# Moving the loads of the stacked Q and K pieces from the SP queue to GpSimd's queue

## The reference

```
L0:  xn  = layernorm(x) * (1 + scale(t)) + shift(t)          scale, shift from the step's embedding
     q,k,v = xn@Wq+bq, xn@Wk+bk, xn@Wv+bv                    16 heads of 16
     s   = q k^T / 4 + attention_bias ; s = -inf where masked; p = softmax(s)
     x1  = xn + (p v)@Wo + bo
     x   = x1 + gelu2(layernorm(x1)*g2+beta2 @ W1 + b1) @ W2 + b2
L1, L3: down projection to 64, gelu, expert matrix chosen per batch element, up projection, residual, layernorm
L2:  rotation of neighbouring features by theta and phi
```

## Time and profile before

| | |
|---|---|
| median of 3 runs | 1190.88 us (1186.92 to 1195.05) |
| profiled execution | 1190.11 us, span 1188.2 us |
| granted TensorE clock | 0.954 |
| busy: PE, DVE, ACT, POOL | 1038.0 (87%), 819.3 (69%), 782.7 (66%), 350.5 (29%) us |
| transfers | 209.41 MB, mean 176 GB/s |

### The profile page before, as it was taken

How to read it: one execution, slowest core, us unless ns; L and a number is a source line. 1 busy time by engine, 2 the same in 40 slices (tenths; PEclk the granted TensorE clock), 3 DMA queues, 4 the chain that set the end, 5 groups by cost and what they waited for, 6 DMA issues and landing times. The chain is left out here.

```text
span 1188.2 us, 22037 instructions
## 1 busy us (share of the span) xinstructions
PE 1038.0 (87%) x6042; PEld 668.8 (56%) x6128; DVE 819.3 (69%) x2056; ACT 782.7 (66%) x1238; POOL 350.5 (29%) x464
## 2 busy tenths in 40 slices
PE   2689999989989989989999999795699998898863
PEld 2446556545645555645654565453577776776641
DVE  5666786776767667758667675674546788978665
ACT  2477887877778778768777786674445656656432
POOL 0205115113212221411511321001555456645421
PEclk9889999999999999999998999898799999999966
DMA  6576986977895896796797696843111101101001
GB/s 229 182 251 203 317 250 217 319 210 237 266 277 187 249 316 219 204 313 217 229 315 212 227 275 172 296 145 121 39 36 36 36 18 53 44 27 36 18 18 36
DMA packets 119913, 209.41 MB, mean 176 GB/s; under 512 B 19104, under 2 KB 46624, under 8 KB 115744
## 3 DMA queue, kind: packets, MB, share of 16 engines
q1 hardware_dynamic: 119840, 208.63, 55.9%
HBM read 187.62 MB, written 20.97 MB: 176 GB/s over the span
## 5 line engine op out<-in xcount | busy, mean ns | idle before, releaser
L690 DVE CUSTOM_DVE_ANT_0 prob<-s_bank,big 128x512 f32<-128x512 f32 x512 | 346.0, 688 | 178.7 <-PE s_bank L549 127.4
L835 ACT ACTIVATE prob<-prob,nmax 128x512 f32<-128x512 f32 x512 | 363.9, 724 | 80.1 <-DVE nmax L690 75.9
L558 PEld LDWEIGHTS t_bank<-ident,prob 128*128 128x128 f32 x2048 | 240.3, 142 | 212.2 <-issue 80.8
L558 PE MATMUL t_bank<-ident,prob 128*128 128x128 f32 x2048 | 320.9, 280 | 10.9 <-ACT prob L835 4.6
L842 ACT COPY pt<-t_bank 128x512 f32<-128x512 f32 x320 | 184.9, 578 | 93.2 <-PE t_bank L558 90.7
L548 PE MATMUL s_bank<-stack_k,stack_q 128*128 128x512 bf16 x426 | 163.9, 385 | 28.1 <-DVE nmax L690 28.1
L549 PE MATMUL s_bank<-mterm_early,ident_bf 128*128 128x512 bf16 x448 | 172.0, 384 | 6.5 <-DMA stack_k<-pieces_dram 2.1
L699 DVE COPY pt<-t_bank 128x512 f32<-128x512 f32 x192 | 132.2, 688 | 41.1 <-PE t_bank L558 41.1
L571 PE MATMUL o_bank<-pt,val 128*32 128x512 f32 x1024 | 140.3, 623 | 0.7 <-ACT pt L842 0.7
L1639 POOL TENSOR_TENSOR gl<-big,gh 128x512 fp32r<-128x512 f32 x64 | 87.2, 1373 | 86.7 <-DVE gh L1344 86.7
L954 POOL TENSOR_SCALAR val<-vst 128x64 f32<-128x64 f32 x128 | 27.0, 244 | 287.7 <-PE o_bank L571 250.1
(11 more groups left out here) (176 smaller groups left out, 1624.1 us busy)
## 6 DMA issues: line engine op xcount, KB each, us to landing
big<-in_fside_Bx16xSxS SPq DMA_DIRECT2D x128, 1024.0 KB, 6.7
stack_q<-pieces_dram SPq DMA_DIRECT2D x128, 128.0 KB, 5.4
stack_k<-pieces_dram SPq DMA_DIRECT2D x128, 128.0 KB, 5.0
pieces_dram<-pieces SPq DMA_DIRECT2D x32, 384.0 KB, 7.1
xin<-in_x SPq DMA_DIRECT2D x8, 512.0 KB, 6.0
x_dram<-x SPq DMA_DIRECT2D x8, 512.0 KB, 3.0
big<-x_dram SPq DMA_DIRECT2D x8, 512.0 KB, 3.3
x1r<-x_dram SPq DMA_DIRECT2D x8, 512.0 KB, 4.4
```

The lines of the kernel that those rows point to most:

```text
L558: last = pe.transpose(t_bank[n % 2][:, c * P:(c + 1) * P], prob[:, n % NT, c * P:(c + 1) * P], ident[:])
L690: dve.tensor_tensor_reduce(out=prob[:, n % NT, :], in0=s_bank[n % 3][:, :], in1=bias[:, h % NB, t, :], scale=-1.0, scalar=3e38, op0=ALU.ad ...
L835: act.activation(tile, tile, ACT.Exp, bias=nmax[:, n % NT:n % NT + 1], scale=-1.0).then_inc(exped.sem, 1)
```

## The change

`load_stack` moves from SP's program to GpSimd's. It now issues one load of Q and one of K per call, and is called behind eight steps in a row: for half 0 behind steps 42 to 49 of the same iteration, for half 1 behind steps 4 to 11 of the next. In the prologue all 16 loads of half 0 come before the first copies of the values, and the 16 of half 1 after them. The waits are the same as before, on GpSimd's queue. SP keeps the stores of the pieces and all other transfers, in their old order.

```diff
--- before.py
+++ after.py
@@ -214,7 +214,8 @@
 TWO_PI_PARTS = (_c1, _c2, 2 * np.pi - _c1 - _c2)
 
 
-HEADS_OF_LOADS = dict(x1=2, expert=4, mask=5, store_0=7, store_1=11, stack_0=9)
+HEADS_OF_LOADS = dict(x1=2, expert=4, mask=5, store_0=7, store_1=11)
+STACKS_FROM = (42, 4)
 STATISTICS_AT, DEVIATION_AT, NORMALISE_AT = 11, 12, 14
 WEIGH_AFTER = 17
 CONTEXT_AFTER = 21
@@ -440,19 +441,6 @@
                     apart(sp, sp_apart)
                     sp.dma_start(pieces_dram[:, qk, c], pieces[:, qk, :, :]).then_inc(pieces_out[c][qk].sem, 16)
 
-            def load_stack(b, c, first=False):
-                if not first:
-
-                    sp.wait_ge(scored.sem, scored.at(b, STEPS // 2 * (c + 1)))
-                    apart(sp, sp_apart)
-                for qk, (stack, piece) in enumerate(((stack_q, QPIECE), (stack_k, KPIECE))):
-                    sp.wait_ge(pieces_out[c][qk].sem, pieces_out[c][qk].at(b, 16))
-                    apart(sp, sp_apart)
-                    for i in range(NP8):
-                        src = pieces_dram[:, qk, c, piece[i]].rearrange("(e h) t -> e h t", e=HD)
-                        sp.dma_start(stack[i::NP8, c * HC:(c + 1) * HC], src
-                                     ).then_inc(stack_in[c].sem, 16)
-
             def store_x1(b):
                 sp.wait_ge(x1_done.sem, x1_done.at(b, DC))
                 apart(sp, sp_apart)
@@ -493,14 +481,9 @@
                         store_pieces(b, 0)
                     if h == HEADS_OF_LOADS["store_1"] and not last:
                         store_pieces(b, 1)
-                    if h == HEADS_OF_LOADS["stack_0"] and not last:
-                        load_stack(b, 0)
-                if not last:
-                    load_stack(b, 1)
 
             for c in range(DC):
                 store_pieces(-1, c, first=True)
-                load_stack(-1, c, first=True)
                 if c == 0:
                     load_x(0)
             iteration(0, first=True)
@@ -974,6 +957,17 @@
                     mterm_late[:, t, :], mraw[:, t, :], MASKED, 0.0, ALU.mult, ALU.add
                 ).then_inc(late_term.sem, 1)
 
+            def load_stack(b, c, i, first=False):
+                if i == 0 and not first:
+
+                    pool.wait_ge(scored.sem, scored.at(b, STEPS // 2 * (c + 1)))
+                for qk, (stack, piece) in enumerate(((stack_q, QPIECE), (stack_k, KPIECE))):
+                    if i == 0:
+                        pool.wait_ge(pieces_out[c][qk].sem, pieces_out[c][qk].at(b, 16))
+                        apart(pool, pool_apart)
+                    src = pieces_dram[:, qk, c, piece[i]].rearrange("(e h) t -> e h t", e=HD)
+                    pool.dma_start(stack[i::NP8, c * HC:(c + 1) * HC], src).then_inc(stack_in[c].sem, 16)
+
             def keep_residual(b, first=False):
                 pool.wait_ge(xt_done.sem, xt_done.at(b, DC))
                 if not first:
@@ -987,6 +981,10 @@
                         copy_values(b - 1, NG - 1)
                     if n == RESIDUAL_AT and not first:
                         keep_residual(b - 1)
+                    if not last and 0 <= n - STACKS_FROM[0] < NP8:
+                        load_stack(b, 0, n - STACKS_FROM[0])
+                    if not first and 0 <= n - STACKS_FROM[1] < NP8:
+                        load_stack(b - 1, 1, n - STACKS_FROM[1])
                     if not last and n in CUT_STEPS:
                         cut(b, CUT_STEPS.index(n))
                     if not last and n in VALUES_AT:
@@ -1001,8 +999,12 @@
             for t in range(QT):
                 early_mask_term(-1, t, first=True)
             pool.wait_ge(consts, 3)
+            for i in range(NP8):
+                load_stack(-1, 0, i, first=True)
             for g in range(NG):
                 copy_values(-1, g, first=True)
+            for i in range(NP8):
+                load_stack(-1, 1, i, first=True)
             keep_residual(-1, first=True)
             iteration(0, first=True)
             before = links[0]
```

## The result

The changed kernel takes 1195.16 us (median of 20 runs, 1191.54 to 1200.28), the kernel before 1191.25 beside it: a ratio of 1.0036 [1.0023, 1.0049]. The forecast was 1178. The time went up by 4 us instead of down by 13. The profiled execution of after took 1200.28 us, 5.1 above its median (span 1198.4, mean clock 0.949 against 0.954), so its traces overstate the difference: 10.2 us between the spans.

The account below looks back on a forecast made before the run. TensorE was busy 95 of 100 us; late transfers cost only by stopping TensorE, VectorE or ScalarE. From 1190.11 us, +6.9 - 3.3 + 3 - 11.5 - 7.5 = -12.4 gave 1178; 8-in-10 range 1162 to 1205.

Parts of the forecast that it names:

- Part 6: Loop's jump back: with two stack loads there instead of sixteen, five stalls each shrink 1.5 us, -7.5 (0 to -26).
- Part 5: Last iteration: SP's late loads start earlier, the bias of head 4 lands in time, with clock gain -11.5 us.
- The floor of 1.5: Jump back: guessed shortest stall, 1.5 us, for a free instruction fetch; no row supported it.
- The 1.6 us of clock: Jump back: TensorE's clock at 0.59 over 4 us after the pause, a loss of 1.6 us each that might be recovered.
- the sign by which the prediction was to fall: Prediction falls altogether if TensorE waits for the stack at step 61, or late loads still delay the last iteration's bias.
- Part 1: GpSimd's queue: price of issuing one stack load, taken as 0.95 us, with ends 0.6 and 1.3.
- c: Time GpSimd needs to issue one stack load, forecast 0.95 us, ends 0.6 and 1.3.
- Rival (b): GpSimd issues as quickly as SP, 0.63 us a load: 1170 us; chance 0.18.
- (a): GpSimd issues slowly, 1.16 us a load, so VectorE waits for the residual copy: 1199 us; chance 0.20.
- (d): GpSimd's descriptors wait for VectorE's SBUF-only work, up to 4 us in each of six iterations: 1202 us; chance 0.05.
- Part 2: Prologue: fifteen issues in a row delay first scores, +6.9 us; SP freed, iteration 0's bias wait goes, -3.3.
- Parts 3 and 4: Loop: half-0 issues at steps 42 to 49 hidden; half-1 at steps 4 to 11 tight, allowance +3 us over six iterations.

Follow-up runs that it names:

- a_from6: Changed kernel with GpSimd's half-1 stack loads behind steps 6 to 13 instead of 4 to 11: 1185.40 us, 0.9949 of the kernel before.
- b_spread: Kernel before, with the 21 late loads spread three each behind heads 5 to 11 of the last iteration: 1181.42 us, ratio 0.9922.
- a_spread: Changed kernel with the 21 late loads spread over heads 5 to 11 of the last iteration: 1188.63 us, 0.9976 of the kernel before.
- a_stack16: Changed kernel with GpSimd's half-1 stack loads from step 16 on instead of step 4: 1186.10 us, 0.9966 of the kernel before.
- a_pro: Changed kernel with SP waiting in the prologue for stack 0 before loading x and storing the second pieces: 1192.32 us, 1.0021 of the kernel before.
- a_best: Changed kernel with half-1 stack loads behind steps 6 to 13, late loads spread, SP waiting for stack 0 in the prologue: 1177.51 us, 0.9886 of before.
- b_xearly: Kernel before, with SP's load of x issued ahead of the 16 half-1 stack loads instead of behind: 1196.28 us, ratio 1.0039.
- a_nobias: Changed kernel without the bias loads after the first four heads, whose bias is used again: 1162.82 us, one run.

## Why the prediction was wrong

Against the profiled executions, forecast and trace by stretch:

| stretch | forecast | trace |
|---|---|---|
| to the first jump back | +6.9 - 3.3 - 1.5 + 0.5 = +2.6 | -0.5 |
| first to last jump back | -4 x 1.5 + 4 x 0.5 = -4.0 | +9.4 |
| last jump to the end of the bias wait | -11.5 + 0.5 = -11.0 | -1.2 |
| the rest | 0 | +2.4 |
| sum | -12.4 | +10.2 |

By the medians the change cost 4 us where 12.4 were to be gained. Two steps make up the miss: Part 6, 13.4 us in the traces from the first to the last jump, of which up to 6 can be chance, and Part 5, 9.8 us.

**Part 6, the jump back, is the first step that failed.** Its premise, that load over the jump lengthens the stall, holds: without the bias traffic the stall is 2.6 to 3.3 us. Its inference doesn't, that two stack loads instead of sixteen in the 5 us make the stall 1.5 us shorter. The stalls grew from 4.96-5.42 to 5.60-6.17 us, and with no stack load beside the jump (a_from6) they were 5.01-5.15: SP's sixteen had cost nothing to win back, and the pair cost 0.55 to 1.0 a jump against a_from6. The instruction packet came 2.3-2.7 us into the stall before, 3.2-3.8 after, 2.6-2.8 in a_from6. A longer stall was excluded ("bounded by nothing gained") without a reason. The floor of 1.5 was a guess; 2.6 was measured, with hardly any traffic. The 1.6 us of clock per stall were right in kind, but nothing was won back.

**Part 5, the last iteration, is the second.** The steps on the issuing side were right: the late loads start earlier, the bias of head 4 goes out 10.6 us sooner. The step "even with the 8.6 us it took" failed. The landing was taken from a trace in which SP's queue was alone; with GpSimd's fourteen loads beside it, it took 17.6 us, and 1.4 of the 9.9 us were won. That the late loads still delay this bias was the sign by which the prediction was to fall, and it came in part: they stand ahead of the bias and the fourteen loads beside it, and moving either ends the wait. b_spread, a_spread and a_stack16 show that the wait goes when the late loads or the stack are moved away from that bias; spreading the late loads was worth 0.78% (9 us) before and 0.60% (7 us) after.

**Part 1, the price.** c is 0.48 us, not 0.95, and below the lower end, 0.6. Rival (b), 0.63, was nearest in the price; its time, 1170, was wrong, since it used Parts 5 and 6. Rivals (a) and (d) didn't happen; the issues beside VectorE's statistics take 0.48 as well. Time is lost behind the issue instead, in the landing: for loads in a row the pace is that of the DMA engines, 0.59 us at best, and not that of the issue.

**Part 2, the prologue.** The size was off. +3.67 came where +6.9 was forecast, for another reason: not the fifteen issues (46.74 against 46.32), but 6.3 us of landing against 3.0. a_pro gives 2.1 of it back. (The 6.9 was a slip too: 56.1 less 49.36 is 6.7.) The 3.3 us of iteration 0 came, and some more: the clock was 0.75 over the 16 us behind that wait before, and 1.00 in this stretch after.

**Parts 3 and 4** were right that the loop's issues are hidden, by the work named; at 0.48 the allowance of 3 us wasn't used.

**That a_best reaches the forecast, 1177.5 us against 1178, is luck.** Its stalls (5.03 to 5.15 us) are hardly shorter than before, where the forecast had 7.5 us of gain, and its prologue costs 1.8 us (mask term at 51.11 against 49.36), not 6.9. Most of its gain is that of the spread late loads, which the kernel before has as well without moving a load (b_spread, 0.9922).

Open are five things: which packets stand ahead of the fetch; why the packet came at 2.3 to 2.7 us before although sixteen stack loads were just being issued there, and at 3.0 to 3.4 when x went ahead of them (b_xearly); how long the stall is with neither stack loads nor x beside the jump, which no run has; why the clock fell more often in one trace of the same loop than in another; and the 2.4 us of the rest.

## What to carry to other kernels

A transfer moved to another engine's queue frees issue time, but the DMA engines stay shared: sum up the landing of whatever was issued behind it and is wanted soon, not only the issue. At a jump back of a loop the instruction fetch is one more transfer in that traffic; look for its packet in the DMA view before guessing, and try what happens when single transfers beside it are moved. A queue that issues faster than the DMA engines move gains nothing. A step or two in a schedule can be worth more than the choice of the engine: here 10 us for the same loads two steps later, at the jumps and in the last iteration together. And one trace of each kernel doesn't price a clock: compare with another trace of the same code.

## What the runs showed of the hardware that was not expected

- An issue on GpSimd costs 0.48 us for 128 KB (16 packets of 8 KB and 16 next to empty), less than on SP, 0.62 to 0.63 with the gap. The Trainium skill ("DMA: Bandwidth & Descriptors", Issuing engine by pattern) calls SP's path generally faster. For the issue this trace says otherwise; the landing is longer (6.3 against 5.4 us), but that it is the path's doing is not shown, since the loads pile up at this pace.
- The sixteen DMA engines were full with such loads at 223 GB/s (a_nobias), 0.59 us a load: more than the 0.48 us of GpSimd's issue and less than SP's 0.63.
- A jump back costs 2.6 to 3.3 us with little DMA traffic and 4.9 to 7.2 with it, and the start of the instruction packet in it moves with it (80 stalls).
- TensorE's clock behind a pause was not the same from trace to trace of one loop: over the 4 us behind the five stalls it was 0.69, 0.57, 1.00, 1.00 and 0.50 in before, with stalls of 4.96 to 5.42 us, and 0.68, 0.50, 0.61, 0.50 and 0.57 in b_spread, with 4.87 to 5.79. In after, with 5.60 to 6.17, it was 0.64 and four times 0.50.
